# A patch embedding, attention and mixture-of-experts block on one core: three pairs of images spread to experts 0 and 1 on chip, the last attention step and the tail in another order

## The reference, cut to what matters

```python
h = patches @ conv_w + conv_b + pos
h = h + attention(layernorm(h))                      # 12 heads of 64, causal, within an image
x = layernorm(h)
top_p, top_i = top_k(softmax(x @ gate_w.T), 2);  w = top_p / sum(top_p)
pos = running count of earlier choices of the same expert, over tokens in order
keep = pos < 245                                     # capacity
buf[expert, pos] = x                                 # kept rows
z = rmsnorm(2 * buf) * norm_w
y = buf + (silu(z @ w1.T) * (z @ w3.T)) @ w2.T       # 512 hidden features
out = h + sum over the two choices of w * keep * y
```

## Time and profile before

| | us |
|---|---|
| median of 3 runs (lowest, highest) | 202.75 (200.14, 203.56) |
| the profiled execution | 200.91 |
| its span, first to last instruction | 198.7 |
| PE busy | 186.6 (94%) |
| DVE busy | 126.3 (64%) |
| ACT busy | 92.1 (46%) |
| POOL busy | 66.7 (34%) |

### The profile page before, as it was taken

The page is one execution under the profiler, slowest core; times in us unless marked ns, Lnnn a source line. Parts: engine busy times, 40 slices in busy tenths (PEclk is TensorE's granted clock), DMA queues, the critical chain, the costliest instruction groups (busy, mean ns, idle before and its releaser), DMA issues.

```text
span 198.7 us, 4906 instructions
## 1 busy us (share of the span) xinstructions
PE 186.6 (94%) x1917; PEld 172.6 (87%) x1918; DVE 126.3 (64%) x385; ACT 92.1 (46%) x190; POOL 66.7 (34%) x106
## 2 busy tenths in 40 slices
PE   7899999999999998999999789999999999999972
PEld 2897998998998997989998664899999999999961
DVE  0268965858482065998896558559458458495363
ACT  2037621135355603284675445658647647643110
POOL 8631500112034000367668533620522523514000
...
GB/s 188 391 401 426 392 247 239 2 38 203 40 0 5 0 0 3 13 23 36 18 38 224 25 13 98 19 52 246 251 152 326 232 178 325 126 31 117 177 68 123
DMA packets 11814, 27.27 MB, mean 137 GB/s; under 512 B 3173, under 2 KB 7108, under 8 KB 10608
## 3 DMA queue, kind: packets, MB, share of 16 engines
...
q10 hardware_dynamic: 512, 0.46, 0.8%
...
## 4 chain that ended last, share of the span: by engine, by line
PE 74%; DMA 10%; DVE 6%; issue 3%; ACT 3%; SPq 1%; POOLq 0%; DVEq 0%; POOL 0%
PE ps L457 8%; PE ps L594 7%; PE ps L427 6%; PE ps L348 4%; PE ps L447 3%; DMA raw<-w_qkv 3%; PE ps L579 3%; PE ps L581 3%; PE ps L575 3%; PE ps L576 3%; PE ps L580 3%; DMA part<-parts 3%; PE ps L405 3%; PE ps L434 3%; DMA xp<-patches 2%
## 5 line engine op out<-in xcount | busy, mean ns | idle before, releaser
L951 POOL DMA_INDIRECT parts<-qT,toke x12 | 17.2, 1431 | 33.2 <-ACT qT L828 31.4
L921 POOL DMA_INDIRECT slots<-row,slot x16 | 16.6, 1039 | 34.6 <-issue 21.8
L1254 DVE TENSOR_TENSOR v<-v,ps 128x246 f32<-128x246 f32 x32 | 12.4, 406 | 16.0 <-ACT v L816 16.0
L1171 DVE TENSOR_TENSOR wqkv<-raw,wqkv 128x1024 fp32r<-128x1024 f32 x16 | 19.5, 1221 | 3.9 <-ACT wqkv L755 3.2
L594 PE MATMUL ps<-xp,v 128*123 128x192 f32 x128 | 22.0, 326 | 0.0
L594 PEld LDWEIGHTS ps<-xp,v 128*123 128x123 f32 x128 | 20.6, 186 | 0.0
L575 PE MATMUL ps<-zeA,wqkv 128*128 128x246 f32 x64 | 18.5, 290 | 0.0
L711 ACT ACTIVATE prob<-sm 128x588 f32<-128x588 f32 x8 | 5.6, 706 | 27.8 <-DVE sm L1010 27.8
L457 PE MATMUL ps<-wo,zs 128*98 128x192 f32 x96 | 17.3, 330 | 1.1 <-ACT zs L721 1.1
L348 PE MATMUL ps<-convw,xp 128*98 128x192 f32 x96 | 17.0, 328 | 0.9 <-DMA xp<-patches 0.9
L579 PE MATMUL ps<-zeA,wqkv 128*128 128x246 f32 x64 | 17.8, 278 | 0.0
...
## 6 DMA issues: line engine op xcount, KB each, us to landing
...
```

The lines of the kernel that those rows point to most:

```text
L951: P.indirect_dma_start(parts, bass.IndirectOffsetOnAxis(toke[:, e, r:r + 1], 0), ye[0:EROWS, e % 2, r, :], None, bounds_check=TOPK * N + E ...
L1171: last = V.tensor_tensor(wsp[:, j, 1, half, :], raw13[j][:, half * W13:(half + 1) * W13], wsp[:, j, 0, half, :].bitcast(f32), ALU.subtract)
```

## The change

In steps 0 to 6 one thing moves: in step 3 PE does `project(2)` before `scores(5)`, not behind it. Step 7 is written out as `last_step`: the first four of the six calls of `project(6)` come before `outputs(7)`, the rest behind it, `transpose_h2(6)` stands in the middle of `project(7)`, and `project(7)` writes to PSUM bank 2, not 6, and follows at once. ACT moves a `split_hi` of 1024 columns from step 6 behind the middle of step 7.

Experts 0 and 1 now get the rows of three pairs (5, 6, 7) on chip. Their loads wait only for the scatters of pairs 0 to 4; the scatter of pair 5 goes behind POOL's last norms and behind the landing of these loads. The stored rows are transposed (one pass, `is_transpose`) ahead of all near rows and open the sum. DVE gets five small operations (`near_slots`) and two more onehots, POOL the first remainder; the filler in step 7 and the nine behind the last count go, and three new ones stand between pair 5's rows and the others. ACT makes `rows(6)` and `rows(7)` later, ahead of `x_hi(0)` and `x_hi(1)`.

`gate_up` starts with the rounded features (it waits for zeA's first half alone), for expert 0 with three of the four column groups. `down(0)` is split around the transposes of expert 2. In the tail only `combine(0)` is before `down(7)`, `weigh_lo(2)` is before `add_part(1, 0)`, and the row numbers of `parts` are permuted so that a partition reads 3072 bytes in one piece.

```diff
+SINCE = PAIRS - 3
...
+        def wo_bank(p):
+            return 6 if p < PAIRS - 1 else 2
+
+        def row_of(p):
+            return p % 2 if p < PAIRS - 1 else 2
...
-            rows_ = parts[k * N + b * n * PT:k * N + (b + 1) * n * PT, :]
-            engine.dma_start(part[:, k, b * n:(b + 1) * n, :], rows_.rearrange("(p q) d -> q p d", q=PT)).then_inc(ld_part[k][b], 16)
+            rows_ = parts[k * N:(k + 1) * N, :].rearrange("(q p) d -> q p d", p=PAIRS)
+            engine.dma_start(part[k][:, b * n:(b + 1) * n, :], rows_[:, b * n:(b + 1) * n, :]).then_inc(ld_part[k][b], 16)
...
-                    sp.wait_ge(scattered[a][k], 16 * (PAIRS - 2) // 2)
+                    sp.wait_ge(scattered[a][k], 16 * ((SINCE + 1 - a) // 2))
...
+            def project(p, some=range(HP)):
+                if 0 in some:
+                    pe.wait_ge(z_ready, p + 1)
+                    if 1 <= p < PAIRS - 1:
+                        pe.wait_ge(h2T_ready, p)
+                    pe.wait_ge(h_ready, PAIRS)
+                for c in some:
+                    last = mm(ps[0:PT, wo_bank(p), 0:D], zs[:, p % 2, c, :], wo[:, c, :], start=(c == 0), stop=(c == HP - 1))
+                if HP - 1 in some:
+                    last.then_inc(wo_done, 1)
...
+            def last_step(s):
+
+                transpose_p(s)
+                logits(s - 2)
+                project(s - 1, range(4))
+                outputs(s)
+                project(s - 1, range(4, HP))
+                count_before(s - 2)
+                project(s, range(3))
+                transpose_h2(s - 1)
+                project(s, range(3, HP))
+
             for s in STEPS:
+                if s == PAIRS - 1:
+                    last_step(s)
+                    continue
...
+                if s == PH - 1:
+                    project(s - 1)
...
-                if in_pairs(s - 1):
+                if in_pairs(s - 1) and s not in (PH - 1, PAIRS):
...
-                if PAIRS - 1 <= s < PAIRS + 2:
-                    keep_busy((1, 3, 9)[s - PAIRS + 1], 3)
+                if s >= PAIRS:
+                    keep_busy((3, 0)[s - PAIRS], 3)
...
+                soon = 3 if e == 0 else 1
+
+                def bank(jt, u):
+                    return ps[:, 2 + jt, u * EC:(u + 1) * EC], slice(u * HID + 128 * jt, u * HID + 128 * (jt + 1))
+
+                def rounded(jt, u):
+                    o, w = bank(jt, u)
+                    mm(o, wsp[:, j, 0, 0, w], zeA[:, j, 0, :], start=(u == 0), stop=False)
+                    mm(o, wsp[:, j, 1, 0, w], zeA[:, j, 0, :], start=False, stop=False)
+
+                pe.wait_ge(zahi_ready, e + 1)
                 pe.wait_ge(elo_ready, e + 1)
-                for jt in range(JT):
+                for jt in range(soon):
                     if e >= 1:
                         pe.wait_ge(hT_ready, JT * (e - 1) + jt + 1)
                     for u in range(2):
-                        o = ps[:, 2 + jt, u * EC:(u + 1) * EC]
-                        w = slice(u * HID + 128 * jt, u * HID + 128 * (jt + 1))
-                        mm(o, wsp[:, j, 0, 0, w], zeA[:, j, 0, :], start=True, stop=False)
-                        mm(o, wsp[:, j, 1, 0, w], zeA[:, j, 0, :], start=False, stop=False)
+                        rounded(jt, u)
...
+                            pe.wait_ge(zalo_ready, e + 1)
+                        mm(o, wsp[:, j, 0, 0, w], zeA[:, j, 1, :], start=False, stop=False)
                         if jt == 0 and u == 0:
                             pe.wait_ge(zelo_ready, e + 1)
...
-                    mm(ps[0:DR, e, EC + c:EC + c + EROWS], xe[0:EROWS, e, r, DA:D], ident[0:EROWS, 0:EROWS], start=False, stop=False)
-                    mm(ps[:, e, c:c + EROWS], xe[0:EROWS, e, r, 0:DA], ident[0:EROWS, 0:EROWS], start=False, stop=False)
-
-            def remainder_rows(e):
-
-                for p in (PAIRS - 2, PAIRS - 1):
-                    spread(nearlo, p, e, end=(p == PAIRS - 1))
+                    mm(ps[:, e, c:c + EROWS], xe[0:EROWS, e, r, 0:DA], ident[0:EROWS, 0:EROWS], start=(r == 0), stop=False, is_transpose=True)
+                    mm(ps[0:DR, e, EC + c:EC + c + EROWS], xe[0:EROWS, e, r, DA:D], ident[0:EROWS, 0:EROWS], start=False, stop=False, is_transpose=True)
...
+            for e in range(NEAR):
+                spread(nearlo, SINCE, e)
+            keep_busy(3, 3)
+            for p in (PAIRS - 2, PAIRS - 1):
+                rounded_rows(p)
+            for p in (PAIRS - 2, PAIRS - 1):
+                pe.wait_ge(nearlo_ready, p - PAIRS + 3)
+                for e in range(NEAR):
+                    spread(nearlo, p, e, end=(p == PAIRS - 1))
...
+                if e == 0:
+                    down(e, (0,))
                 pe.wait_ge(ld_e[e % 2], 16 * (e // 2 + 2))
                 pe.wait_ge(zelo_ready, e + 1)
                 transpose_x(e + 2, e % 2)
-                down(e)
+                down(e, (1,) if e == 0 else range(2))
...
-            for i in range(2):
-                combine(i)
+            combine(0)
             down(EXPERTS - 1)
-            for i in range(2, len(ONCHIP)):
+            for i in range(1, len(ONCHIP)):
...
-                    act.wait_ge(bscale_ready, p - 1)
+                    act.wait_ge(slot_ready, p - 1)
...
+                if s == PAIRS - 1:
+                    weigh_second(s - 2)
                 if in_pairs(s):
                     outputs(s)
+                if s == PAIRS - 1:
+                    near_rows(nearhi, SINCE).then_inc(nearhi_ready, 1)
+                    near_rows(zlast, SINCE).then_inc(zlast_ready, 1)
                 if in_pairs(s - 1):
                     transposed_h2(s - 1)
-                if in_pairs(s - 2):
+                if in_pairs(s - 2) and s < PAIRS - 1:
                     weigh_second(s - 2)
                 if in_pairs(s - 3):
                     bases_of(s - 3)
-                if PH - 1 <= s < PAIRS - 1:
+                if PH - 1 <= s < PAIRS - 2:
                     split_hi((s - PH + 1) // 2, (s - PH + 1) % 2)
+                if s == PAIRS - 1:
+                    split_hi(1, 1)
...
-            bases_of(PAIRS - 3)
-            for p in (PAIRS - 2, PAIRS - 1):
-                weigh_second(p)
             for p in (PAIRS - 2, PAIRS - 1):
                 near_rows(nearhi, p).then_inc(nearhi_ready, 1)
             for p in (PAIRS - 2, PAIRS - 1):
                 near_rows(zlast, p).then_inc(zlast_ready, 1)
             for p in (PAIRS - 2, PAIRS - 1):
-                rows(p)
+                weigh_second(p)
...
-            for e in range(2):
+            for e in range(NEAR):
+                rows(PAIRS - 2 + e)
...
-            scatter(PAIRS - 3)
+            pool.wait_ge(nearhi_ready, 1)
+            pool.wait_ge(zlast_ready, 1)
+            P.tensor_tensor(nearlo[:, 0, :], zlast[:, 0, :], nearhi[:, 0, :].bitcast(f32), ALU.subtract).then_inc(nearlo_first, 1)
             scales2_last()
             for e in range(NEAR):
                 pool.wait_ge(ld_e[e], 16)
+            scatter(PAIRS - 3)
...
-                base_scales(r)
-
-            def place_last():
+                if r < PAIRS - 3:
+                    base_scales(r)
+
+            def near_slots():
+
+
+                a = SINCE % 2
+                then(V.tensor_tensor(slotw_of[:], slotf[:, a, :], far[:, a, :], ALU.add))
+                V.tensor_scalar(above_of[:], slotw_of[:], float(STRIDE), FAR, ALU.is_lt, ALU.mult)
+                then(V.tensor_tensor(nearat_of[:, 0:1], slotw_of[:, 0:1], slotw_of[:, 1:2], ALU.min))
+                then(V.tensor_tensor(above_of[:], above_of[:], slotw_of[:], ALU.add))
+                return mark(V.tensor_tensor(nearat_of[:, 1:2], above_of[:, 0:1], above_of[:, 1:2], ALU.min))
+
+            def mark_place(p, e, at):
+                V.tensor_scalar(onehot[:, p - SINCE, e, :], places_row[:, e, :], at, None, ALU.is_equal).then_inc(onehot_ready, 1)
...
+                for e in range(NEAR):
+                    mark_place(SINCE, e, nearat_of[:, e:e + 1])
...
+                for p in (u, w):
+                    dve.wait_ge(nearhi_ready, p - SINCE + 1)
+                    dve.wait_ge(zlast_ready, p - SINCE + 1)
+                    V.tensor_tensor(nearlo[:, p - SINCE, :], zlast[:, p - SINCE, :], nearhi[:, p - SINCE, :].bitcast(f32), ALU.subtract).then_inc(nearlo_ready, 1)
...
+                if s == PAIRS - 1:
+                    residual_and_choose(-1, s - 2)
+                    residual_and_choose(s - 1, -1)
...
-            for r in (PAIRS - 2, PAIRS - 1):
+            for r in range(SINCE, PAIRS):
...
+            weigh_lo(2)
             add_part(1, 0)
-            weigh_lo(2)
+            weigh_lo(3)
...
-    row_of = np.arange(TOPK * N, dtype=np.float32).reshape(TOPK, PAIRS, PT).transpose(2, 1, 0)
-    number = np.stack([row_of, row_of % N], axis=-1).reshape(PT, 2 * TOPK * PAIRS)
+    row_of = np.arange(TOPK * N, dtype=np.float32).reshape(TOPK, PT, PAIRS).transpose(1, 2, 0)
```

127 lines of the change are left out of this document (64 added, 63 removed).

## The result

The changed kernel takes 199.13 us in the median of 20 runs (197.87 to 202.55), the kernel before 202.87 us on the same chip (20 runs, 199.52 to 203.60). The ratio is 0.9879 with a 95% interval of 0.9844 to 0.9914: 2.5 us gained, where 5.2 were forecast, and less than the 2% from which the prediction spoke of faster (it gave 0.25 to a time within 2%). The medians are 3.7 us apart; the ratio leaves out as slow every run over 1.5% above the fastest of its kernel, which are 14 of the 20 before (202.67 to 203.60) and 3 of the 20 after. The profiled execution took 199.29 us, its span is 197.5 (before 200.91 and 198.7).

What follows compares the result with a forecast made beforehand. The prediction took PE as the bound, busy for 186.6 of 198.7 us. Its terms, 0.8 + 1.3 + 1.9 + 1.2 = 5.2 us, came off the median of 202.75 us to give 197.5, range 194.2 to 200.9.

Steps and rivals of the forecast that it cites:

- expert 2's stage: Scatters, slot loads and transposes for expert 2: all in time for PE, nothing lost, split of down(0) costed at nothing.
- step 7: PE's new order around outputs(7) and project(7): h2 of pair 7 earlier by 1.3 us, bounds 0.3 and 2.3.
- the first rival: The stall in outputs(7) comes again whole and the tail's parts land as before: 3.5 us gained, 199.2 us; chance 0.20.
- the stall: In outputs(7), ACT released 2.97 us after the small matmuls' start, cause unknown; step 7 gains 2.3 us without it, 0.3 with it.
- Step 3: project(2) fills PE's wait ahead of scores(5): 0.8 us gained, bounds 0.3 and 0.9.
- h2(7) to gate_up(0): From pair 7's residual to the first gate_up: 8.3 us instead of 10.2, 1.9 gained, bounds 1.2 and 2.3.
- Tail: After down(7): no PE wait before the last combine and parts landing sooner, 1.2 us gained, bounds 0.5 and 1.4.

Runs made afterwards that it cites:

- e7: The kernel before with only project(2) moved ahead of scores(5) in step 3; ratio 0.9975 to the kernel before.
- e2: The kernel before with SyncE's load of expert 3's first weights, w13(3), moved ahead of the wait for all scatters; fast chip, ratio 0.9943.
- e3: The changed kernel with GpSimd's scatter of pair 4 held until outputs(7) is done, on a fast chip; ratio 0.9919 to the kernel before.
- e14: The changed kernel with GpSimd's scatter of pair 4 held until outputs(7) is done, on a slow chip; 197.66 us, ratio 0.9796 to the kernel before.
- e13: The changed kernel again, unchanged, on a slow chip; 200.65 us, ratio 0.9875 to the kernel before.
- e15: The changed kernel with the 10 fillers at the start written as 40 shorter ones, shifting PE's stream by 60 instructions; slow chip, 198.70 us, ratio 0.9815.
- e5: The changed kernel, unchanged, on a fast chip; ratio 0.9852 to the kernel before.
- e18: The kernel before with only GpSimd's scatter of pair 4 held until outputs(7) is done; slow chip, ratio 1.000.

## Why the prediction was wrong

Two steps of the sum failed: expert 2's stage was put at nothing and lost 1.9 us, and step 7 was put at 1.3 and won 0.17. The median of 199.13 us is that of the first rival, "the stall and the parts stay" (199.2). Its four terms are in the two first profiles as it put them (0.66 + 0.17 + 2.09 + 0.56 = 3.5), but so are the 1.9 us lost at expert 2, which it put at nothing too; and 2.1 us lie between the profiles and the medians, which no term has. That the median meets it is luck.

**Step 3, 0.8 (bounds 0.3 and 0.9).** "count_before(1) waits for it" stood in the text with its row, and the sum took 0.8 nevertheless. PE had no work between the new place of its wait and the next use, so the gain ended there: 0.0 on fast chips (e7, e2 against e3). The 0.66 of the two first profiles are a stall in outputs(3) that the new wait covers; that it is near 0.8 is luck.

**Step 7, 1.3 (bounds 0.3 and 2.3).** The step that failed is "neither end is nearer; I take the middle". The whole stall came again, 0.17 were won, and the first rival had priced this. Shown for outputs(7) (e14 against e13 and e15, one profile each): with the scatter beside it this stream of small matmuls is reported 2.5 us late on a slow chip, with the scatter held it isn't. For the rest it is what overlaps: outputs(3) comes 0.6 and outputs(6) 0.3 us later on slow chips than on fast chips, both beside a scatter, and outputs(4) and (5), beside none, don't. The trace of before had these rows. Whether it is GpSimd's own work or the transfers that it starts was not tried. Without the stall, on a fast chip, the whole change of step 7 is worth 0.7. So the upper bound, 2.3, counted as gain of the order what is mostly gain of the stall's absence.

**h2(7) to gate_up(0), 1.9.** Right: 2.09 in the first profiles, 2.08 between e2 and e5. Transposes for products, the fillers left out, and gate_up on zeA alone do together what they should; none was tried apart.

**"Expert 2 ... Nothing is lost."** The largest miss: a term put at nothing that measured -1.9. Two things. Its loads of slots were followed and found in time, as they were; but the order of SyncE was followed no further than slots(2): w13(3) is queued behind all of them, is issued at 135.24 as before (135.14), and the stage ahead now needs it 2 us sooner. This costs 1.4 (tr(3) to tr(4) 8.93, before 7.57). The rest, 0.5, is tr(2) to tr(3), 6.64 us where half a down less makes 6.15: expert 2's operands go through ACT and DVE, PE has one half of down(0) less to cover them and waits (0.4 us of it for zeA's remainder). "PE's 4.6 us per gate_up cover them" was not checked against that. Where the weights land in 4.9 us, only the second is lost: gate_up(0) to tr(4) is 24.90 in e5 and 24.31 in e2.

**Tail, 1.2 (bounds 0.5 and 1.4).** 0.56 between the two first profiles. PE waits no more, and DVE's split stands in the idle time ahead of the second part: from that part to the first sum 3.18 us in place of 3.54. But the term took 0.7 for an earlier landing, and 0.2 of it came in this pair (5.76 us in place of 5.99). The row was there: 193 GB/s at a share of 0.67 says that the engines stood idle for a third of the time, so that shorter packets could not be all of it. Of the rule on small descriptors (the Trainium skill, "DMA: Bandwidth & Descriptors", "Why small descriptors are slow (HBM only)"), from which I had estimated half a microsecond, the traces can neither confirm nor refute the size: profiles of one layout differ among themselves by up to 0.9 us.

This pair of profiles is not the whole of it, though. From tr(7) to the end the four profiles with the old tail take 24.02, 24.33, 25.45 and 26.13 us (before, e2, e7, e18), the fifteen with the new tail and layout 22.58 to 24.78, in the mean 23.5: 1.5 us less, which is more than the term. What parts the first two from the last two is the granted clock, and no term had it; the last section shows it.

**The sum** of what the parts are worth: on a fast chip 0 + 0.7 + 2.1 - 0.6 + 0.4 to 1.5 (tails of e2 and e7 against e5) = 2.6 to 3.7, measured 2.9 (e5); on the first chip 0.66 + 0.17 + 2.09 - 1.9 + 0.56 = 1.6 in the profiles, 2.5 by the ratio, 3.7 by the medians. The profiled execution of before, 200.91 us, is like the 6 of its 20 runs that took under 202 us. What the other 14 lost is not in these terms; the last section has a candidate.

That the scatter of pair 4 should be held is not shown. e14 has the lowest ratio of all, 0.9796 on a slow chip against e13's 0.9875, but with 4 runs, an interval that reaches 0.9876, and a gate_up(0) only 0.2 us sooner than in after. On a fast chip nothing speaks for it (e3 0.9919, e5 0.9852 on another).
